# Joined decays in the state-space stage, and the second normalisation inside the projections

## What is computed

```python
# state space, per direction, chunks of 128 tokens
Y_diag = einsum('bcln,bcsn,bhcls,bcshp->bclhp', C, B, Lmat, x * dt)  # Lmat: decay from s to l
Y_off  = einsum('bcln,bchpn,bhcl->bclhp', C, states, exp(A_cs))
y = rms(silu(z) * (Y_forward + Y_backward + x * (D + fc_D(x)))) @ out_proj
# layer 1
xn = layernorm(x + gate * ys)
q, latent = xn @ Wq, (xn @ Wk + xn @ Wv) @ W_down_kv
k, v = latent @ W_up_k, latent @ W_up_v
logits = xn @ router_w
```

## Time and profile before

| what | us |
|---|---|
| median of 3 runs (lowest, highest) | 1984.8 (1983.58, 1989.7) |
| the profiled execution | 1983.85 |
| its span, first to last instruction | 1982.2 |
| loop of the state-space stage, one sequence | about 70 |
| second normalisation, first DMA to barrier | 977.8 to 1034.7 |
| projections | 1034.7 to 1154.4 |

### The profile page before, as it was taken

How to read it: one execution, slowest core, us unless ns; L and a number is a source line. 1 busy time by engine, 2 the same in 40 slices (tenths; PEclk the granted TensorE clock), 3 DMA queues, 4 the chain that set the end, 5 groups by cost and what they waited for, 6 DMA issues and landing times. The chain is left out here.

```text
span 1982.2 us, 33791 instructions
## 1 busy us (share of the span) xinstructions
PE 1776.8 (90%) x10009; PEld 1227.8 (62%) x10090; DVE 1379.6 (70%) x3026; ACT 1185.7 (60%) x2870; POOL 429.3 (22%) x406
## 2 busy tenths in 40 slices
PE   5689999999999799999578879999989898989897
PEld 2456766676676689999433455656556464656555
DVE  3867887877788222222256978888879797888885
ACT  5256666566556222122154448887888888888886
POOL 2032442353244304321120120110202010020101
PEclk9789999999999999999789979999999999999999
DMA  5511222222121496554284752242425232343311
GB/s 177 191 54 64 95 95 73 80 101 74 63 95 64 174 318 204 196 180 148 83 283 134 213 164 75 78 83 76 107 76 107 70 90 62 84 98 85 88 27 33
DMA packets 149694, 226.12 MB, mean 114 GB/s; under 512 B 17613, under 2 KB 118095, under 8 KB 149424
## 3 DMA queue, kind: packets, MB, share of 16 engines
q1 hardware_dynamic: 132928, 189.39, 31.1%
q0 software_dynamic: 16624, 35.01, 7.3%
HBM read 174.26 MB, written 50.99 MB: 114 GB/s over the span
## 5 line engine op out<-in xcount | busy, mean ns | idle before, releaser
L2390 DVE TENSOR_SCALAR att_scores<-att_psS 128x512 f32<-128x512 f32 x512 | 349.1, 682 | 95.8 <-PE att_psS L2220 57.4
L2339 ACT ACTIVATE att_prob<-att_scores,att_shift 128x512 f32<-128x512 f32 x512 | 383.6, 749 | 24.4 <-DVE att_shift L2406 24.3
L2348 ACT COPY att_pT<-att_psT 128x512 f32<-128x512 f32 x512 | 306.3, 599 | 134.3 <-PE att_psT L2228 133.5
L2398 DVE CUSTOM_DVE_ANT_0 att_scores<-att_scores,first_decay 128x512 f32<-128x512 f32 x512 | 347.9, 680 | 0.0
L2228 PEld LDWEIGHTS att_psT<-ident,att_prob 128*128 128x128 f32 x2048 | 244.3, 141 | 158.8 <-issue 98.2
L2228 PE MATMUL att_psT<-ident,att_prob 128*128 128x128 f32 x2048 | 314.4, 277 | 19.4 <-ACT att_pT L2348 16.0
L2220 PE MATMUL att_psS<-first_ks,first_qs 128*128 128x512 bf16 x431 | 165.0, 384 | 15.5 <-DVE att_scores L2390 13.2
L2242 PE MATMUL att_psO<-att_pT,att_v 128*32 128x512 f32 x1024 | 139.2, 618 | 42.3 <-ACT att_pT L2348 37.9
L1614 ACT ACTIVATE ffn_hT<-ffn_psH,ffn_b 128x128 f32<-128x128 f32 x156 | 44.6, 368 | 194.2 <-PE ffn_psH L1570 194.1
L1166 ACT ACTIVATE mamba_L<-mamba_am,mamba_minus 128x128 f32<-128x128 f32 x512 | 153.1, 387 | 0.1
L1570 PE MATMUL ffn_psH<-ffn_xT,ffn_w 128*128 128x128 f32 x1248 | 146.1, 275 | 6.0 <-DMA ffn_w<-in_w 5.4
(11 more groups left out here) (314 smaller groups left out, 2850.5 us busy)
## 6 DMA issues: line engine op xcount, KB each, us to landing
ffn_w<-in_w SPq DMA_DIRECT2D x47, 1024.0 KB, 5.8
mamba_am<-a_rows SPq DMA_DIRECT2D x64, 512.0 KB, 3.8
first_qs<-q_parts SPq DMA_DIRECT2D x256, 64.0 KB, 3.0
first_ks<-k_parts SPq DMA_DIRECT2D x256, 64.0 KB, 3.1
xn<-xn_all SPq DMA_DIRECT2D x16, 512.0 KB, 6.0
att_w<-in_inter POOLq DMA_DIRECT2D x7, 1024.0 KB, 5.5
att_w<-in_outer POOLq DMA_DIRECT2D x7, 1024.0 KB, 6.8
q_parts<-proj_parts SPq DMA_DIRECT2D x8, 768.0 KB, 4.1
```

Of the source, the lines that this page charges most:

```text
L2339: nc.scalar.activation(prob[:, n % NP], scores[:, n % NCL], ACT.Exp, bias=shift[:, h % 2, t:t + 1], accum_out=total[:, octet % 2, t, j, i: ...
L2348: nc.scalar.copy(pT[:, h % HEADS_T, :, t * P:(t + 1) * P], bank_of("turn", n)[:].rearrange("p (k q) -> p k q", k=CPB)).then_inc(pT_ready, 1)
L2390: vec.tensor_scalar(scores[:, n % NCL], psS[n % NS][:], -CLAMP, CLAMP, ALU.max, ALU.min).then_inc(clipped, 1)
L2398: vec.tensor_tensor_reduce(scores[:, n % NCL], scores[:, n % NCL], decay[:, FAR - t * P:FAR - t * P + SEQ], 1.0, -2.0 * CLAMP, ALU.mult, A ...
```

## The change

State space: the logarithm of the step goes into `minus` (so the exponential holds decay and step together), the clamp moves from 1.0 to 3.0e38, and `xdt` is gone: PE multiplies with the rows `xl` themselves. NL is 6. DVE's `decays(t)` does both directions of a tile and adds them in a new pass; PE's `diagonal(t)` is one set of 8 products a tile, preceded by `neighbours(t)` and followed by `off(t)` for both directions. ACT makes all 8 decays in one run ahead of the squares. `finish` is split into `take_tile` and the rest, and the product with the gate moves from DVE to POOL. In `route_and_steps` ACT takes one more logarithm, DVE one more clamp.

Layer 1: `normalise_and_project` takes the place of both stages. The rows go through rings (4 slots of x, got and xn, 6 of xT), the router's product is made per batch with xT as the stationary operand, moments(0) to (2) stand ahead of the loop and the others in batches 0 to 2, the router's steps two to three batches later, the table's steps at the end, and all eight `multiply` quarters behind PE's loop. The table's large tiles lie in the tiles of the rows.

```diff
-    NA, NL = 4, 4
+    NA, NL = 4, 6
...
+                v.tensor_scalar(w[:], steps.dt[:], LEAST_NORMAL, None, ALU.max).then_inc(floored, 1)
...
-                v.tensor_copy(steps.minus[:].rearrange("p d t h -> p (d t h)"), psM[:].rearrange("p d n -> p (d n)")).then_inc(minus_ready, 1)
+                dve.wait_ge(logged, 2)
+                v.tensor_tensor(steps.minus[:].rearrange("p d t h -> p (d t h)"), psM[:].rearrange("p d n -> p (d n)"),
+                                lw[:].rearrange("p d t h -> p (d t h)"), ALU.add).then_inc(minus_ready, 1)
...
+                    def diagonal(t):
+                        pe.wait_ge(L_ready, i * CPB + t + 1)
+                        for h in range(NH):
+                            mm = nc.tensor.matmul(psY[t % 2][:, h * HD:(h + 1) * HD], L[:, 2 * t % NL, h], xl[:, t, h * HD:(h + 1) * HD],
+                                                  start=False, stop=(h == NH - 1), skip_group_check=True)
+                        mm.then_inc(diag_used, 1)
+                    def off(t):
+                        pe.wait_ge(state_ready, (i + 1) * 6)
+                        for d in range(2):
+                            if (d == 0 and t > 0) or (d == 1 and t < CPB - 1):
+                                done = max(2 * t - 2 + d, 0) if t else 0
+                                pe.wait_ge(off_scaled, i * 6 + done)
+                                lo = t * P + (0 if d == 0 else 2)
+                                nc.tensor.matmul(psO[d][:], xc[:, 5 + 2 * d, lo:lo + P], state[:, d, t],
+                                                 start=True, stop=True).then_inc(off_ready, 1)
...
+                    neighbours(0)
                     diagonal(0)
+                    products(2)
+                    neighbours(1)
+                    diagonal(1)
+                    off(0)
+                    off(1)
+                    products(3)
+                    neighbours(2)
+                    diagonal(2)
+                    off(2)
+                    turn_tile(0)
+                    neighbours(3)
+                    output(0)
+                    diagonal(3)
+                    off(3)
+                    turn_tile(1)
+                    output(1)
                     turn_tile(CPB - 2)
...
-                    for u in range(NL):
+                    for u in range(U):
                         decays(i, u)
-                    decays(i, 4)
                     squares(i, 0)
...
+                    def gate(t):
+                        pool.wait_ge(summed, i * CPB + t + 1)
+                        nc.gpsimd.tensor_tensor(y[:, t % 2], y[:, t % 2], zs[:, t], ALU.mult).then_inc(gated, 1)
+                    skip_rows(0)
+                    skip_rows(1)
+                    gate(0)
+                    skip_rows(2)
+                    rms(0)
+                    gate(1)
+                    skip_rows(3)
+                    rms(1)
+                    gate(2)
+                    rms(2)
+                    gate(3)
+                    rms(3)
...
+                    def decays(t):
+                        dve.wait_ge(g_ready, i * CPB + t + 1)
+                        dve.wait_ge(L_masked, i * U + (2 * t - 2 if t >= 2 else 0))
+                        v.tensor_tensor(masked[:, t % 2], gT[t % 2], C.triangles[:], ALU.mult).then_inc(g_masked, 1)
+                        dve.wait_ge(g_masked, i * CPB + t + 1)
+                        for d in range(2):
+                            u = 2 * t + d
+                            dve.wait_ge(decayed, i * U + u + 1)
+                            v.scalar_tensor_tensor(out=L[:, u % NL], in0=L[:, u % NL], scalar=LARGE,
+                                                   in1=masked[:, t % 2, d].unsqueeze(1).to_broadcast([P, NH, P]),
+                                                   op0=ALU.min, op1=ALU.mult).then_inc(L_masked, 1)
+                        dve.wait_ge(L_masked, i * U + 2 * t + 2)
+                        v.tensor_tensor(L[:, 2 * t % NL], L[:, 2 * t % NL], L[:, (2 * t + 1) % NL], ALU.add).then_inc(L_ready, 1)
...
                     decays(0)
-                    decays(1)
                     dve.wait_ge(fd_done, (i + 1) * CPB)
                     dve.wait_ge(xfd_ready, i * CPB)
                     v.tensor_tensor(fd[:], fd_ps, d_bc[:].unsqueeze(1).to_broadcast([P, CPB, NH]), ALU.add).then_inc(fd_ready, 1)
+                    decays(1)
                     grow(2)
+                    take_tile(0)
+                    decays(2)
                     count = 0
+                    for t in range(CPB):
+                        count = off(2 * t, count)
+                        count = off(2 * t + 1, count)
+                        if t:
+                            take_tile(t)
+                        finish(t)
+                        if t == 1:
+                            decays(3)
+                        elif t >= 2:
+                            outputs(t - 2)
```

The joined stage, its PE list and the core of SP's and DVE's:

```diff
+                def store_rows(b):
+                    sp.wait_ge(merged, (b + 1) * CPB)
+                    sp.dma_start(rows(out_d, b), x[:, b % NR]).then_inc(x_kept, 16)
+                    sp.wait_ge(xn_ready, (b + 1) * CPB)
+                    sp.dma_start(rows(xn_d, b), xn[:, b % NR]).then_inc(xn_kept[b % NR], 16)
+                    sp.wait_ge(x_kept, (b + 1) * 16)
+                    if b + NR < BATCH:
+                        load_rows(b + NR)
...
+                keep_running(nc, C, psL[:, 0:P], 30)
...
+                turn(0, 0)
+                turn(1, 0)
                 latent(0)
                 pe.wait_ge(w_in, 3 * 16)
                 for b in range(BATCH):
                     queries(b)
+                    if b == 0:
+                        router_products(0)
+                    if NORMS[b]:
+                        turn(2 * b + 2, b)
+                    if 1 <= b <= 3:
+                        router_products(2 * b + 1)
+                    elif b == 0:
+                        router_products(1)
                     keys(b)
                     if b + 1 < BATCH:
                         latent(b + 1)
                     values(b)
-                    if b == 2:
+                    if NORMS[b]:
+                        router_products(2 * b + 2)
+                        turn(2 * b + 3, b + 1)
+                    if b == 5:
                         router.ranks(pe)
-                    elif b == BATCH - 2:
-                        table.multiply(nc, pe, psR[:, 0:2 * table.columns], 0, 0)
...
+                for k in range(2):
+                    for q in range(4):
+                        table.multiply(nc, pe, psR[:, 0:2 * table.columns], k, q)
...
+                moments(0)
                 dve.wait_ge(kvd_in, 3 * 16)
                 v.tensor_tensor(wkT[:], wkT[:], wvT[:], ALU.add).then_inc(joined, 1)
+                moments(1)
                 dve.wait_ge(wkv_made, 1)
                 v.tensor_copy(wkv[:].rearrange("p k n -> p (k n)"), psV[0][:, 0, 0:KD * LAT]).then_inc(wkv_ready, 1)
+                moments(2)
...
                         take(Q, b)
+                    if b < 3:
+                        moments(2 * b + 3)
                     if b:
                         subtract(K, b - 1)
                         take_low(Q, b - 1)
...
                         take(K, b)
+                    if b < 2:
+                        moments(2 * b + 4)
+                    if b < BATCH:
                         subtract(Q, b)
```

More of the change, by code:

```diff
@@ L45 @@
 CLAMP = 10000.0
+LARGE = 3.0e38
 DECAY = 0.01 * 0.01
@@ L1780, in _ @@
                     sp.wait_ge(v_stored[slot], BATCH // 2 * 16)
+                for slot in range(NR):
+                    sp.wait_ge(xn_kept[slot], BATCH // NR * 16)
             @block.tensor
```

324 lines of the change are left out of this document (197 added, 127 removed).

## The result

The changed kernel takes 2005.7 us (median of 4 runs, 2001.1 to 2007.6), the kernel before in the same rounds 1985.0: ratio 1.010, 95% interval 1.0076 to 1.0124. It is slower, by 15 to 25 us; forecast were 1997 (1966 to 2011) and a chance of 0.54 for slower. The prediction's likeliest case had a range of its own, 1990 to 2003, and 2005.7 lies above it. The profiled execution took 2001.09 us (span 1999.3, mean granted clock 0.937), against 1983.85, 1982.2 and 0.963.

What follows compares the result with a forecast made beforehand. PE was taken to bound the state-space loop, DVE after the change; no engine filled the two joined stages. 10.4 + 3 + 0.7 - 2 = 12 us over 1983.85 gave 1996, as a median 1997, range 1966 to 2011.

Steps and rivals of the forecast that it cites:

- likeliest case: Whole kernel: the layout as summed holds, 1990 to 2003 us, chance 0.42.
- the layout: State-space loop: queues laid out by engine; saved 7 us become about 9 of idle PE, 1.3 us more a sequence, 10.4 for 8.
- the sums: State space, DVE: four added sums of both directions' decays, 5 us in front of the last diagonal.
- the blocking: State space: POOL's multiplications hold up DVE's passes where both read SBUF, 4.05 us of blocks in the layout.
- Rival 1: State space: POOL doesn't block DVE, 1.5 us less a sequence, 1971 us in all; chance 0.19.
- The tiny multiplications of rms: State space: by the port rule alone they would block DVE too, some 4 us over 8 sequences; left out of the sum.
- Rival 2: State space: PE stays the bound, the full 7 us a sequence is saved, 1927 us in all; chance 0.05.
- The clock: State space: PE's idles lower its granted clock; bounds 0 and 1.7 us a sequence, 0.4 taken, 3 us in all.
- Rival 4: State space: clock stays low past the waits, 1.7 us a sequence, 1997 + 10, with late queries 2010; chance 0.14.
- The joined stage: Second normalisation and projections in one stage: ends at 1151.5 against 1153.3, 2 us less.
- the slow bound for the tail: Joined stage's end: the table product's eight quarters run at the low clock, 3.5 us each; the full clock was 1.86.
- rival 3: Joined stage's end: tail at full clock, 14 us less from the stage, same state-space loss, 1985 us; chance 0.17.

Runs made afterwards that it cites:

- experiment 4: New state-space stage alone, with the sum of the two directions' decays made for 8 of 1024 columns, against the kernel before: ratio 0.9861.
- experiment 3: New state-space stage alone, with GpSimd's skipped-row multiplications writing one head instead of eight, against the kernel before: ratio 0.9988.
- experiment 5: New state-space stage alone, with VectorE's decays of tile 3 ahead of taking and finishing tile 1, against the kernel before: ratio 1.0041.
- experiment 1: New route-and-steps and state-space stages alone, normalisation and projections kept as two stages, against the kernel before: ratio 1.0067, median 1996.9 us.
- experiment 9: New state-space stage alone, both queues reordered, tile 0's output moved earlier, filling products in TensorE's waits, against the kernel before: ratio 1.0009.
- experiment 11: Joined stage alone, router products with 8 weights stationary and 512 columns moving, turning back left out, against the kernel before: ratio 1.0004.

## Why the prediction was right in sign and short in size

**State space, the layout (10.4 us forecast): right.** The last sum ends at 28.0 (forecast 28.1), the convolutions begin at 34.4 (34.2), waits of 1.98, 2.24 and 1.42 us stand before the first two diagonals and the waiting off-diagonal product (2.1, 2.5, 3.5). The last is smaller because the products ahead of it ran at half speed, not because VectorE was sooner. The step grew by 1.55 us against 1.3 and 0.4 for the clock. Two of its terms were isolated: the sums (experiment 4) and the blocking (experiment 3). What it lacked is that VectorE's path to the last diagonal isn't alone: TensorE's behind the off-diagonal product is as long, as experiment 5 shows. The blocks measured 1.46, 1.59 and 0.2 us, 3.2 where 4.05 were laid out. One thing was over-counted: a last sequence has no convolutions behind it, and was 1.3 us shorter than before. And the first sequence began 1.2 us earlier in this execution, which it did not in experiment 1. So 8.4 in the profiled execution, not 14; the timed rounds of the stage alone say 13 (8 to 19).

**Rival 1, that GpSimd doesn't block: out.** By the Trainium skill ("SBUF — State Buffer", "Who interferes with whom") two inputs in SBUF are what exposes VectorE, and the passes agree (2.36 us a pair alone, 3.82 and 3.95 beside GpSimd's multiplications). The tiny multiplications of rms, which by that rule alone would also have blocked VectorE, did not: the one at 300.58 lasted 1.21 us instead of 0.54 and ended 0.4 us behind the pass that ran when it began, and VectorE's sum behind it ran at its unopposed 1.23. Leaving that out of the sum was right.

**Rival 2, that TensorE stays the bound: out**, and experiment 4 bounds it: even without the sums the step falls by 2.2 us, not 7.

**The clock (3 us forecast, 0.4 a sequence).** It fell in every sequence, as expected, over the 14 us from the second diagonal on, to 0.76 in three of them and to 0.63 in five. The step's growth leaves 0.25 us for it beside the layout's 1.3, so it was mostly hidden behind VectorE, also as expected. With the queues reordered, filling the waits brought 1.3 us a sequence (experiment 9, with what it leaves open).

**Rival 4, that the clock stays low past the waits**, had 2007, nearest to the 2005.7. That is chance: it put 1.7 us on every sequence, which would be masks 73 us apart, and they are 71.65. Where the clock did cost much, in the joined stage, there were no waits.

**The joined stage (-2 forecast): the failing term.** The step that failed was "two turns (1.1 each) and two router products (1.6 each) make it 14.8 for batches 0 to 2", 44.4 us for the three. Two things were wrong in it. Every piece was priced at the full clock; and PE's list in the change has three router products in batch 0, not two, at 1.7 to 1.8 us each. From queries to queries the batches took 25.1, 18.5 and 17.1 us in the changed kernel, and 18.3, 18.1 and 16.7 in the joined stage alone. At a steady full clock (experiment 11) they took 17.0, 15.4 and 16.0, 48.4 in all (60.7 in the changed kernel, 53.0 in the joined stage alone). So 4 us of the shortfall were there at any clock, and the clock added 12 us in the one execution and 5 in the other. The stage of experiment 11 took 175.2, 1.5 us less than the two before, which is within a microsecond of the layout; in part that is luck, as the batches were still 4 us too long and the logits' turning back is left out. I had looked for a low clock only behind idle time, and between these batches there was none. The first take, the price of the quarters and the choice of the slow bound for the tail were right; rival 3, the tail at full clock, is out. The whole shortfall stands ahead of the table's product, which began at 1137.7 (1128.8 in the joined stage alone) instead of 1121.

**In sum**, 12 us were forecast against the profiled execution and 17 came; against the medians it was 12 and 21. The two errors have opposite signs: 14 for the state space where that execution had 8, and -2 for the joined stage where it had 13. In the timed rounds of the parts the sum is 13 and 5. No version that does all the work beat the kernel before; reordered and filled, the state space is level with it, and the joined stage with wide router products, whose turning back would still have to be paid, is too.

## What to carry to other kernels

Halving the bound engine's work is worth nothing if the sum that makes it possible goes to the next engine's queue ahead of the same point: lay out that queue first, with what another engine's SBUF reads add to it. Count TensorE's pieces in the new list, and price them by what stands next to them, not by their best row: here groups of products with 8 columns moving were enough for a low clock though the engine never stopped, and turning them so that the long side moves held it. And moving one group in a balanced pair of queues mostly moves the wait: of four orders tried, two changed nothing clear of the noise and two lost, one of them only by its traces; one of the first two reached the time before, together with filling products.

## What the runs showed of the hardware

The granted clock fell while TensorE was busy 10.00 us of 10 as the profile counts it (0.60, then 0.50), behind 32 instructions of 8 columns, and did not fall with the same work as groups of 4 instructions of 512 columns (1.00 in four windows running). The Trainium skill ("TensorE: Matmul & The Clock Gate", "Part 1: The HAM clock gate (the "warmup" mystery)") ties the clock to how busy the engine has been and treats idle time as what lowers it; in these rows products back to back were not enough when they were narrow. How long the clock then stays low differs between two executions of the same stage code: behind the first router products it was 0.50 for some 20 us (1019 to 1039) in the changed kernel, and the stage took 189.4 us; in the joined stage alone it was low for some 3 us (1011 to 1014) and back at 1.00, and the stage took 180.5. Seventeen filling products a sequence (34 instructions in the trace, 4 us of TensorE's time) held the clock at 1.00 over 20 us, with waits of up to 2.05 us in them, in four of the eight sequences; in the others it was 0.91 or 0.93 there.
